# Rows 24 to 27 of o from TensorE to GpSimd and VectorE in a triangular solve, and another order of the Q columns

## The reference, cut to what matters

```python
def step(Sst, inp):
    qt, kt, vt, bt, gt = inp
    Sd = gt[..., None, None] * Sst
    kS = jnp.einsum('bhk,bhkv->bhv', kt, Sd)
    Snew = Sd + jnp.einsum('bhk,bhv->bhkv', kt, bt[..., None] * (vt - kS))
    ot = jnp.einsum('bhk,bhkv->bhv', qt, Snew)
    return (Snew, ot)
```

## Time and profile before

| what | us |
|---|---|
| median of 3 runs | 1049.38 |
| the runs | 1047.09, 1054.67, 1049.38 |
| the profiled execution | 1052.18 |
| span of its instructions | 1050.5 |
| busy: PE, DVE, ACT, POOL | 805.0, 674.9, 379.1, 247.1 |
| mean granted TensorE clock | 0.863 |

### The profile page before, as it was taken

The page is one execution under the profiler, slowest core; times in us unless marked ns, Lnnn a source line. Parts: engine busy times, 40 slices in busy tenths (PEclk is TensorE's granted clock), DMA queues, the critical chain, the costliest instruction groups (busy, mean ns, idle before and its releaser), DMA issues.

```text
span 1050.5 us, 21523 instructions
## 1 busy us (share of the span) xinstructions
PE 805.0 (77%) x8645; PEld 617.5 (59%) x8645; DVE 674.9 (64%) x961; ACT 379.1 (36%) x550; POOL 247.1 (24%) x192
## 2 busy tenths in 40 slices
PE   4756954879987745766394899228999997999997
PEld 2434734864534533544184888116887785888885
DVE  4583786668885684877848985553567663455454
ACT  5334653630201112641362231525565631222232
POOL 5000693004899401004500000311333310000000
PEclk9977976889999866987886766759999999999999
DMA  7000000020000000000100000213444422222221
GB/s 259 1 1 1 2 1 2 2 82 0 1 0 1 0 1 0 1 1 0 32 2 2 4 4 3 75 47 105 147 151 140 157 86 61 68 68 59 69 67 49
DMA packets 21189, 46.05 MB, mean 44 GB/s; under 512 B 2498, under 2 KB 6882, under 8 KB 20740
## 3 DMA queue, kind: packets, MB, share of 16 engines
q1 hardware_dynamic: 21124, 45.11, 13.9%
HBM read 43.73 MB, written 1.37 MB: 43 GB/s over the span
## 4 chain that ended last, share of the span: by engine, by line
PE 55%; DVE 15%; ACT 3%; issue 3%; POOL 2%; DMA 1%; DVEq 0%; ACTq 0%; POOLq 0%
PE psum L1535 10%; PE psum L1534 9%; PE psum L1533 9%; PE psum L1678 5%; PE psum L1688 4%; PE psum L709 4%; PE psum L710 3%; PE psum L711 3%; PE psum L1817 2%; DVE arena L1344 1%; DVE arena L1426 1%; DVE arena L1425 1%; POOL arena L834 1%; DVE arena L1394 1%; PE psum L1727 1%
## 5 line engine op out<-in xcount | busy, mean ns | idle before, releaser
L1533 PE MATMUL psum<-xh,arena 128*128 128x296 f16 (+1 forms) x664 | 196.7, 296 | 27.3 <-DVE arena L1442 9.7
L1534 PE MATMUL psum<-xl,arena 128*128 128x296 f16 (+1 forms) x664 | 196.7, 296 | 0.0
L1535 PE MATMUL psum<-xh,arena 128*128 128x296 f16 (+1 forms) x664 | 196.3, 296 | 0.0
L1533 PE MATMUL psum<-arena 37*64 37x17 f16 (+5 forms) x1116 | 115.4, 209 | 46.7 <-DVE arena L1106 15.7
L1533 PEld LDWEIGHTS psum<-arena 37*64 37x64 f16 (+5 forms) x1116 | 92.2, 120 | 53.7 <-issue 32.2
L1534 PE MATMUL psum<-arena 37*64 37x17 f16 (+5 forms) x1116 | 114.9, 207 | 2.4 <-issue 2.4
L1535 PE MATMUL psum<-arena 37*64 37x17 f16 (+5 forms) x1116 | 114.7, 207 | 2.5 <-issue 2.5
L632 DVE TENSOR_TENSOR arena<-psum,arena 128x592 f32<-128x592 f32 x68 | 52.7, 775 | 87.3 <-PE psum L1535 70.0
L1534 PEld LDWEIGHTS psum<-arena 37*64 37x64 f16 (+4 forms) x1116 | 93.1, 122 | 6.4 <-issue 2.9
L1535 PEld LDWEIGHTS psum<-arena 37*64 37x64 f16 (+4 forms) x1116 | 92.9, 121 | 4.8 <-issue 1.3
L709 PE MATMUL psum<-arena 128*128 (+3 forms) x340 | 92.8, 273 | 3.6 <-DVE arena L640 3.6
(11 more groups left out here) (298 smaller groups left out, 1645.5 us busy)
## 6 DMA issues: line engine op xcount, KB each, us to landing
arena<-comb SPq DMA_DIRECT2D x68, 296.0 KB, 3.4
arena<-in_wmoe SPq DMA_DIRECT2D x34, 384.0 KB, 3.1
arena<-in_xt SPq DMA_DIRECT2D x4, 864.0 KB, 9.5
arena<-in_w SPq DMA_DIRECT2D x2, 1024.0 KB, 6.6
arena<-in_ctrl SPq DMA_DIRECT2D x1, 1056.0 KB, 9.6
out<-arena SPq DMA_DIRECT2D x2, 512.0 KB, 3.2
arena<-in_wlin SPq DMA_DIRECT2D x1, 768.0 KB, 4.7
arena<-in_wqkv SPq DMA_DIRECT2D x1, 768.0 KB, 4.3
```

The costliest lines, as they stand in the source:

```text
L1533: pe.matmul(dst, wh, mh, start=start, stop=False)
L1534: pe.matmul(dst, wh, ml, start=False, stop=False)
L1535: return pe.matmul(dst, wl, mh, start=False, stop=stop)
```

## The change

Only the solve's Q side is changed. `QROWS` goes from 24 to 28, so that rows 24 to 27 of o are made by products on GpSimd and sums on VectorE, no longer by Q columns and TensorE. The two PSUM banks now hold rows 28 to 31 and 32 to 36, and a column has 64 * 9 = 576 numbers until x passes 28. The function `q_until` is written anew: 23 columns for every 25 rows until row 27 (0 after row 3, 11 after row 15, 19 after row 23, 23 after row 27), then 14 columns for every 9 rows. The square inside the loop moves from row 28 to row 32, and the two parts of the norm are split at 28.

```diff
-QGROUPS = [3, 4]
-QROWS = GROUPS[QGROUPS[0]][0]
+QPARTS = [(28, 32), (32, S)]
+QROWS = QPARTS[0][0]
 OPARTS = [0, QROWS, S]
 QWIDE = 64 * (S - QROWS)
...
 def q_until(s_):
-    if s_ >= 24:
-        return min(s_ + 1, 18 + ((s_ - 23) * 19 + 12) // 13)
-    return max(0, 9 * (s_ - 3) // 10)
+    if s_ >= QROWS:
+        return min(s_ + 1, 23 + ((s_ - QROWS + 1) * 14 + 8) // 9)
+    return max(0, 23 * (s_ - 2) // 25)
...
-            for i, g in enumerate(QGROUPS):
-                t0, t1 = GROUPS[g]
+            for g, (t0, t1) in enumerate(QPARTS):
                 act.wait_ge(ev["qadded"], t1)
...
-            oq = [fill(("oq", g)) for g in QGROUPS]
+            oq = [fill(("oq", g)) for g in range(len(QPARTS))]
...
-                    for bk, g in zip(oq, QGROUPS):
-                        g0, g1 = GROUPS[g]
+                    for bk, (g0, g1) in zip(oq, QPARTS):
                         t0 = max(x, g0)
                         if x < g1:
```

More of the change, by code:

```diff
@@ L133, in plan_tiles @@
         place[("R", g)] = (len(place), "row", GROUPS[g][1])
-    for g in QGROUPS:
+    for g in range(len(QPARTS)):
         add(("oq", g), "oq")
@@ L1322, in _ @@
                 if i:
-                    dve.wait_ge(ev["oread"], len(QGROUPS))
+                    dve.wait_ge(ev["oread"], len(QPARTS))
                 dve.tensor_reduce(oms[:, 0, tj].rearrange("p (t j) -> p t j", j=HJ), osq[:, ts], AX, ALU.add).then_inc(
@@ L1331, in _ @@
                 if i:
-                    dve.wait_ge(ev["ocopy"], len(QGROUPS))
+                    dve.wait_ge(ev["ocopy"], len(QPARTS))
                 dve.tensor_tensor(o[:, ts], o[:, ts], oms[:, 0, tj].rearrange("p (t j) -> p t j", j=HJ).unsqueeze(
```

## The result

| | before | changed |
|---|---|---|
| median of 20 runs, us | 1047.19 | 1051.21 |
| the profiled execution, us | 1052.18 | 1050.89 |
| span, us | 1050.5 | 1049.2 |
| first copy of u, us from the start of the span | 232.56 | 228.94 |
| from there to the copy of the last five rows of o | 122.3 | 124.4 |

The account below looks back on a forecast made before the run. Bound by TensorE until row 16, then GpSimd, then both: -2.3 + (49.0 - 33.6) + (14.2 + 1.5 - 28.0) + 1.6 - 0.3 = +2.1 us, median 1051.5 us, 8-in-10 range 1046 to 1057.

Parts of the forecast that it names:

- To row 16: Solve up to row 16, TensorE the bound: smaller Q columns bring the copy of row 16 2.3 us earlier.
- Row 16 to the last product: GpSimd the bound: with four more products and four more columns, 49.0 us without a gap against 33.6.
- The third rival: Rows 26 to 29: VectorE's new sums become the bound, up to 7.3 us, median 1058.8 us; chance 4%.
- The drain: Q columns left after the last product: 15 instead of 20, 14.2 us plus 1.5 of waits, against 28.0.
- The first rival: After the last product TensorE is the bound and its savings come through: -6.7 us, median 1042.7; chance 10%.
- The second: TensorE from row 28 stays at 1.2 GHz: all the drain, median 1059.4 us (3%); half, 1054.4 (11%).
- The tail: Norm behind the solve: second part shrinks from 832 to 576 elements, first grows; -0.3 us in all.
- The signs: Listed trace checks; first copy of u to last Q addition should differ from 122.2 us by -3 to +6.
- The clock's 1.6 us: Start of the drain: TensorE again at 1.2 GHz after mostly idle rows, charged 1.6 us; ends 0 and 9.4.
- the wait of 1.86: Kernel before, 331 to 333 us: GpSimd's wait for TensorE at the lower clock, 1.86 us.
- the 28.0 us of before: Kernel before: time from the last product's end to the last column's end, with 3.4 us of waits for TensorE.
- rule on idle gaps: Gaps between matmul bursts lower TensorE's clock repeatedly; added rows with 3 us gaps would cost 1.6 us.

Follow-up runs that it names:

- short_products: Changed kernel with GpSimd's products of rows 24 to 27 cut to 8 of their 25 to 28 columns (stale sums): 1041.0 us, ratio 0.9938 to before.
- after_warm: Changed kernel plus eight spare matmuls that change no result behind the columns of each of rows 22 to 28: ratio 1.0006 to before, solve 123.0 us.
- before_warm: Kernel before plus eight spare matmuls that change no result behind the columns of each of rows 22 to 24: ratio 1.0015, solve 120.6 us.
- before_warm2: Kernel before plus eight spare matmuls that change no result behind the columns of row 24 alone: ratio 1.0001, solve 121.1 us.
- order_only: Kernel before, QROWS still 24, with only the changed kernel's order of the Q columns: ratio 0.9991, solve 122.7 us.
- table_only: Kernel before with a q_until table handing TensorE two to three columns a row in rows 20 to 24, all columns on GpSimd: ratio 0.9995.
- late_table: Kernel before with a q_until table holding back columns of rows 17 to 21 until after row 25, all on GpSimd: ratio 0.9956, solve 118.4 us.

## Why the prediction was right, and where its size was off

It forecast +2.1 us; in the profiled executions the solve and its tail are 1.9 us longer (124.4 against 122.3, and 5.7 against 5.9 from the copy of o to the quantising). The medians say +4.0. The range held both.

- *To row 16.* Forecast 2.3 us earlier. The copy of row 16 comes 56.2 us after the first copy of u and not 58.3: 2.0.
- *Row 16 to the last product.* Forecast 49.0 us without a gap, 3.73 us for the last product. Measured 336.22 - 287.11 = 49.1, and 3.75. VectorE's sums were hidden: it still waited 1.93 us for the last product. The third rival is out.
- *The drain.* Forecast 14.2 + 1.5 + 1.6 + 0.5 = 17.8 us; measured 353.3 - 336.2 = 17.1, of which waits for TensorE 2.9 (forecast 3.1).
- *The first rival,* TensorE the bound of the drain: out by short_products. *The second,* the lower clock for half of the drain or all: 0.50 and 0.77 in its first 8 us, so less than half.
- *The tail.* Forecast -0.3, measured 5.7 - 5.9.

- *The signs.* From the first copy of u to the last Q addition it is 2.1 us more than before, where -3 to +6 was allowed. The wait at row 32 fell to 4.85 us ("about 4"), and 15 columns stood behind the last product.

The clock's 1.6 us, which the prediction called its unknown, came out at 1.4: that much the changed kernel's drain loses when its first wait is 2.53 and not 1.11 us (after_warm). The kernel before pays as much in its own profile, 1.7 us against before_warm, and there too the prediction had it right: it left the wait of 1.86 in the 28.0 us of before.

The size is off in the timed runs alone. They say 4.0 us by the medians, 2.5 to 4.9 by the interval of the ratio, and the sum of 2.1 lies just below that. No experiment found the other 2 us. One reading is that most executions of the kernel before don't pay the low stretch that its profile shows; without it the same sum would give 2.1 + 1.6 = 3.7. For it speaks that before_warm is no faster in the timed runs. Against it speaks that the profiles of before_warm2, order_only and table_only, all with `QROWS` 24 and every column on GpSimd, have a low stretch near there too: 0.63 from 322 to 326 us in before_warm2, whose code is that of before up to that point, 0.50 from 322 to 330 in order_only and from 326 to 328 in table_only. Only before_warm, with its spare matmuls, and late_table, with its own order, have none. How much of the stretch lies in the drain differs from one to the other. Another reading is that the 2 us lie outside the solve, where the profiles differ by more than that. Which of them holds stays open. That the forecast's size met the profiled difference to 0.2 us is in part luck, since such a difference moves by 1 us or more from one execution to the next.

The Trainium skill's rule on idle gaps ("TensorE: Matmul & The Clock Gate", section on HAM oscillation) was weighed and thought to be worth 1.6 us against this change. The trace agrees with its sign: 0.54 over the 15 us in which GpSimd alone set the pace, and the fall came inside an idle gap (shown at the end).

## What to carry to other kernels

Moving a sum from one engine to another moves its multiplications as well, or leaves them where they were; count the queue that stays the same first. Here 6784 multiplications stayed on GpSimd, the engine that had no idle time, and of the 11 us that TensorE was to save only 2.0 came through, up to row 16; behind it the saving lay beside GpSimd's queue as idle time, in which the clock fell. Where three engines take turns as the bound, ask which one is waiting in the stretch that sets the end (VectorE, 1.2 to 1.9 us a row for each of the last five products of the changed kernel) and give it whole pieces of the full one's work. And read a stage from its own first instruction: the two profiled spans of this case had the sign wrong through a stage that nobody touched.

## What the runs showed that I had not expected

Spare matmuls that change no result made the changed kernel faster, by 2.3 to 3.0 us in the timed runs and 1.4 to 1.5 us in the profiled solve. Eight of them, 1.95 us in the trace, in each row of 4.6 us held the granted clock at 1.00 where it had been 0.54. Without them the clock fell in the middle of a wait. Over the whole row TensorE was busy more than half of the time, but all of that lay in its first part:

```profile
310.00:314.60 4.60, 2.47 (x9) 1.27 (x7) 2.71 (x4) 0.32 (x1) 4.60 (x4) 0.99 0.00 0
314.60:318.00 3.40, 2.15 (x5) 1.58 (x6) 2.25 (x6) 0.32 (x1) 3.40 (x2) 0.50 0.00 0
```
```profile
311.34 1.13 PE L1686 MATMUL psum<-arena,ident 128*128 128x256 f32 x4
315.85 1.43 PE L1677 MATMUL psum<-arena 128*128 128x320 f32 x2 [3.38 <-DVE arena L455]
```

TensorE ended its work at 312.47 us and had been idle for 2.1 us when the clock fell, at about 314.6. It then stayed at 0.50 until about 328, although the waits of the next rows were only 1.0 to 1.3 us long.
